# Attention mixing turned round: probabilities as the moving operand, value tiles of 32 columns for four heads held stationary, denominators from a ones tile, inverted by Ln and Exp on ScalarE

## The reference

```python
qk = einsum('bceqd,bcekd->bceqk', q, k) / sqrt(h)
a = softmax(qk, axis=-1)
o = einsum('bceqk,bcekd->bceqd', a, v)
...
x = x + _conv(_mcl(o, Wo, bo), o_conv_w, o_conv_b, 0)
```

## Time and profile before

| | us |
|---|---|
| median of 3 runs | 1269.8 (1269.31 to 1272.35) |
| profiled execution | 1263.9 |
| its span | 1262.0 |
| PE busy | 1106.7 |
| DVE busy | 965.2 |
| POOL busy | 874.2 |
| ACT busy | 655.4 |

### The profile page before, as it was taken

How to read it: one execution, slowest core, us unless ns; L and a number is a source line. 1 busy time by engine, 2 the same in 40 slices (tenths; PEclk the granted TensorE clock), 3 DMA queues, 4 the chain that set the end, 5 groups by cost and what they waited for, 6 DMA issues and landing times. The chain is left out here.

```text
span 1262.0 us, 30504 instructions
## 1 busy us (share of the span) xinstructions
PE 1106.7 (88%) x12696; PEld 752.7 (60%) x12696; DVE 965.2 (76%) x1466; ACT 655.4 (52%) x1078; POOL 874.2 (69%) x812
## 2 busy tenths in 40 slices
PE   0299999999893888999999999999999589999997
PEld 0177777777672145666667666666667444455553
DVE  3789899999763998988898888988873385544344
ACT  1555555555332176666666666666666223346345
POOL 0467777777584499988998888988889005947900
PEclk9899999999897599999999999999989899999999
DMA  9825234331654455445352707162000499975661
GB/s 303 254 79 153 87 111 121 98 111 47 139 132 124 66 89 142 69 79 94 81 97 58 122 28 143 34 115 57 27 19 18 130 365 316 269 256 161 194 208 54
DMA packets 137778, 159.30 MB, mean 126 GB/s; under 512 B 17853, under 2 KB 85709, under 8 KB 137641
## 3 DMA queue, kind: packets, MB, share of 16 engines
q1 hardware_dynamic: 113448, 119.37, 38.8%
q10 hardware_dynamic: 15648, 28.81, 6.5%
q0 software_dynamic: 8544, 9.18, 2.7%
HBM read 106.48 MB, written 52.89 MB: 126 GB/s over the span
## 5 line engine op out<-in xcount | busy, mean ns | idle before, releaser
L1106 POOL TENSOR_TENSOR a_pl<-a_prob 128x512 bf16<-128x512 f32 x416 | 452.0, 1113 | 54.8 <-ACT a_prob L1063 50.7
L1063 ACT ACTIVATE a_prob<-a_col 128x512 f32<-128x512 f32 x512 | 303.0, 597 | 187.2 <-PE a_col L953 176.3
L1007 DVE TENSOR_REDUCE a_negmax<-a_row 128x1 f32<-128x512 f32 x512 | 336.6, 694 | 48.1 <-PE a_row L931 47.6
L710 POOL TENSOR_TENSOR f_yl<-f_y,f_yh 128x768 bf16<-128x768 f32 x80 | 132.8, 1679 | 93.0 <-ACT f_yh L657 93.0
L970 PE MATMUL a_mix<-a_vp,a_prob 128*128 128x65 bf16 x2048 | 195.5, 195 | 1.1 <-DVE a_o L1032 0.9
L970 PEld LDWEIGHTS a_mix<-a_vp,a_prob 128*128 128x128 bf16 x2048 | 163.7, 99 | 53.5 <-issue 5.2
L971 PE MATMUL a_mix<-a_vp,a_pl 128*128 128x65 bf16 x2048 | 193.9, 195 | 0.0
L971 PEld LDWEIGHTS a_mix<-a_vp,a_pl 128*128 128x128 bf16 x2048 | 146.4, 99 | 60.4 <-issue 4.4
L657 ACT ACTIVATE f_yh<-f_y 128x768 bf16<-128x768 f32 x80 | 67.4, 844 | 138.9 <-DVE f_y L548 120.2
L450 PE MATMUL f_acc<-f_wh,f_xh 128*32 128x384 bf16 x1280 | 109.9, 332 | 28.0 <-DVE f_wl L538 25.9
L931 PE MATMUL a_row<-k,q 96*128 96x512 bf16 x256 | 108.3, 429 | 29.0 <-PEq L202 15.0
(11 more groups left out here) (153 smaller groups left out, 2356.8 us busy)
## 6 DMA issues: line engine op xcount, KB each, us to landing
X<-b_x ACTq DMA_DIRECT2D x16, 526.0 KB, 8.2
q<-in_x SPq DMA_DIRECT2D x8, 1024.0 KB, 7.5
a_v<-V SPq DMA_DIRECT2D x16, 512.0 KB, 4.4
Z<-a_z ACTq DMA_DIRECT2D x32, 256.0 KB, 2.7
b_z<-Z SPq DMA_DIRECT2D x16, 512.0 KB, 11.2
b_x<-in_x SPq DMA_DIRECT2D x32, 256.0 KB, 9.9
b_res<-X SPq DMA_DIRECT2D x38, 208.0 KB
out<-b_y ACTq DMA_DIRECT2D x38, 208.0 KB
```

The source lines that it names most:

```text
L710: nc.gpsimd.tensor_tensor(yl[half][n % 2][:], y[half][:], yh[half][n % 2][:], ALU.subtract).then_inc(yl_done, 1)
L1007: nc.vector.reduce_max(negmax[u][:, QT * h + qt:QT * h + qt + 1], row[row_buffer(h, qt)][:], AX.X, negate=True).then_inc(max_done, 1)
L1063: nc.scalar.activation(prob[head % PROBS][:, kt, :], col[kt % 2][:], ACT.Exp).then_inc(exp_done, 1)
L1106: nc.gpsimd.tensor_tensor(pl[head % PROBS][:, kt, :], prob[head % PROBS][:, kt, :], ph[head % PROBS][:, kt, :], ALU.subtract).then_inc(lo_ ...
```

## The change

- `mix_step` becomes `mix_set`. A set is one key block of four heads (4 steps). For each head the stationary operand is a 128 x 32 tile, and the 512 probabilities of that key block move. The four heads of a quad write to partitions 0-31, 32-63, 64-95, 96-127 of one PSUM tile. First come 8 matmuls with a tile of ones (ph and pl of four heads) into `weight`, then 12 with values (vh with ph, vl with ph, vh with pl) into `mix`. Four sets make a quad: features of four heads on the partitions, queries along the free axis.
- `weight` and `mix` have one PSUM buffer each; before, `mix` had two.
- DVE's `invert` and `norm` per head become, per quad, Ln of `weight` on ACT (`log_weight`), Exp of its negative (`invert`) and one 128 x 512 multiplication on DVE (`divide`), straight into `oT`. An activation table set with both functions is loaded ahead.
- The product of the low parts (vl with pl) is left out; before, it was made.
- The tail loses the fp32 turn of `o` and the two copies to `oT`: 8 matmul parts instead of 16 and two ACT operations instead of four.
- `split_max` loses its cast: the high part is read in place.
- DVE still makes 6 of 32 low parts, now every fifth step. Slots: `EXP` 42, `MIX` 54, `KEEP` (Ln, Exp, divide) 67 and 83, `TAIL` 85 to 93.
- Steps are ordered so that four heads of a key block follow one another (`tile_of`). Loads, their order and their bytes are unchanged.

```diff
+        mix = ps("a_mix", [P, W])
+        weight = ps("a_weight", [P, W])
...
+        KEEP = MIX + QUAD * (QT - 1) + 1
+        TAIL = KEEP + QUAD * QT + 2
...
+            def mix_set(n, g):
+                kt, quad = g % QT, SETS // QT * n + g // QT
+                p = (SETS * n + g) % RING
+                pe.wait_ge(lo_pool, pool_lows(n, g))
+                pe.wait_ge(lo_dve, dve_lows(n, g))
+                if n == g == 0:
+                    pe.wait_ge(ones_set, 1)
+                if kt == 0 and quad:
+                    pe.wait_ge(logged, quad)
+                for part in (ph, pl):
+                    for r in range(QUAD):
+                        nc.tensor.matmul(weight[r * DH:(r + 1) * DH, :], ones[:], part[p][:, r, :],
+                                         start=kt == 0 and part is ph, stop=kt == QT - 1 and part is pl)
+                if g == 0:
+                    pe.wait_ge(v_lo, n + 1)
+                if kt == 0 and quad:
+                    pe.wait_ge(divided, quad)
+                for j, (vv, part) in enumerate(((vh, ph), (vl, ph), (vh, pl))):
+                    for r in range(QUAD):
+                        h = g // QT * QUAD + r
+                        last = nc.tensor.matmul(mix[r * DH:(r + 1) * DH, :], vv[n % 2][:, kt, h * DH:(h + 1) * DH], part[p][:, r, :],
+                                                start=kt == j == 0, stop=kt == QT - 1 and j == 2)
                 last.then_inc(mixed, 1)
...
-                    if j < FH:
-                        last = nc.tensor.matmul(out[:, at], o[u % 2][:, part, n, j * P:(j + 1) * P], ident[:], start=n == 0, stop=n == 1)
...
+                for f in range(FH):
+                    last = nc.tensor.matmul(out[:, at], wo[n % CHANNELS][:, f, j * P:(j + 1) * P], oT[n % 2][:, f, at], start=f == 0, stop=f == FH - 1)
...
-                nc.vector.tensor_copy(high, negmax[u][:]).then_inc(max_hi, 1)
...
+            def divide(n, m):
+                quad = SETS // QT * n + m
+                if m == 0 and n >= 2:
+                    ve.wait_ge(out_full, FH * (n - 1))
+                ve.wait_ge(mixed, QT * (quad + 1))
+                ve.wait_ge(inverted, quad + 1)
+                nc.vector.tensor_tensor(oT[n % 2][:, m, :], mix[:], inverse[quad % 2][:], ALU.mult).then_inc(divided, 1)
+
+            pipeline(steps(0, row_max) + units(SPLIT, split_max) + lows(EXP + 1, low_part, False) + quads(KEEP, divide))
...
+            act.preload_act_table_set("natural_log_exp_and_others")
...
+            def log_weight(n, m):
+                quad = SETS // QT * n + m
+                act.wait_ge(mixed, QT * (quad + 1))
+                nc.scalar.activation(logs[quad % 2][:], weight[:], ACT.Ln).then_inc(logged, 1)
+
+            def invert(n, m):
+                quad = SETS // QT * n + m
+                act.wait_ge(logged, quad + 1)
+                if quad >= 2:
+                    act.wait_ge(divided, quad - 1)
+                nc.scalar.activation(inverse[quad % 2][:], logs[quad % 2][:], ACT.Exp, scale=-1.0).then_inc(inverted, 1)
...
+            pipeline(quads(KEEP, log_weight) + units(TURN + 1, keep_max) + units(TURN + 2, load_max) + units(EXP - 2, v_high) + steps(EXP, exp) + quads(KEEP, invert)
+                     + tails(TAIL + QT, keep_out) + tails(TAIL + QT + 1, store_z))
```

More of the change, by code:

```diff
@@ L749, in attend @@
         ident16 = sb("a_ident16", [P, P], BF16)
-        o = [sb(f"a_o{s}", [P, QT, 2, F]) for s in range(2)]
+        ones = sb("a_ones", [P, DH], BF16)
         q = [q0, sb("a_q1", [SHIFTED, HEADS, QT, CHANNELS, P], BF16)]
@@ L916, in _ @@
             sp.dma_start(centre[:], T["centre"]).then_inc(mixing_in, 16)
-            for i in range(1, ITERATIONS):
+            for i in range(1, C // CHANNELS):
                 load(i)
@@ L922, in _, with row_scores @@
         def _(pe):
[L923 to L931, removed]
+            def row_scores(n, t):
+                step, s, m = STEPS * n + t, entry(n), n % CHANNELS
+                h, qt = t // QT, t % QT
+                if m == 0 and t % (QT * HALF) == 0:
+                    pe.wait_ge(qk_in[s][h // HALF], 16 * QK_LOADS * (n // PAIR + 1))
+                if step >= ROWS:
+                    pe.wait_ge(max_done, step - ROWS + 1)
+                nc.tensor.matmul(row[step % ROWS][:].rearrange("p (t w) -> p t w", t=QT), q[s][0:QK_ROWS, h, qt, m, :], k[s][0:QK_ROWS, h, :, m, :],
@@ L954, in col_scores @@
                                  start=True, stop=True).then_inc(col_full, 1)
[L956 to L970, removed]
-                    last = nc.tensor.matmul(mix[h % 2][:, qt, :], pl[p][:, kt, at], vpart, start=False, stop=kt == QT - 1)
+            def mix_set(n, g):
[20 more added lines that the diff above has]
+                                                start=kt == j == 0, stop=kt == QT - 1 and j == 2)
@@ L972, in mix_step, with tail @@
                 last.then_inc(mixed, 1)
-            def tail(i, u, j, part):
-                unit = UNITS * i + u
+            def tail(n, j, part):
                 at = slice(part * PART, (part + 1) * PART)
@@ L1000, in _, with row_max @@
             nc.vector.tensor_copy(ident16[:], ident[:]).then_inc(ident16_set, 1)
[L1001 to L1005 removed]
+            nc.vector.memset(ones[:], 1.0).then_inc(ones_set, 1)
+            def row_max(n, t):
+                step = STEPS * n + t
                 ve.wait_ge(row_full, step + 1)
[L1007 removed]
@@ new lines, in load_max, with exp @@
+            def load_max(n):
+                act.wait_ge(max_kept, n + 1)
+                act.dma_start(q[entry(n)][QK_ROWS:SHIFTED, :, :, n % CHANNELS, :], maxrows[n % PAIR][:]).then_inc(max_in[n % PAIR], 16)
+            def exp(n, t):
+                step = STEPS * n + t
+                sets_done = step // QUAD
+                if t % QUAD == 0 and sets_done >= RING:
+                    act.wait_ge(mixed, sets_done - RING + 1)
+                act.wait_ge(col_full, step + 1)
+                nc.scalar.activation(prob[sets_done % RING][:, t % QUAD, :], col[step % 2][:], ACT.Exp).then_inc(exp_done, 1)
@@ L1086, in _ @@
+            for j in range(FH):
+                act.wait_ge(z_stored[j], 16 * UNITS)
         @block.gpsimd
```

283 lines of the change are left out of this document (118 added, 165 removed).

## The result

| | before | after |
|---|---|---|
| median, us | 1270.4 (1269.31 to 1272.35, 4 runs) | 1256.0 (1250.15 to 1258.79, 4 runs) |
| span of the profiled execution | 1262.0 | 1256.9 |
| `front`, to the end of its last engine | 406.5 | 413.1 |
| `attend`, first k block cleared to last store | 587.5 | 570.8 |
| of it: first Exp to last low part | 537.6 | 529.2 |

The ratio is 0.9879 (95% 0.9841 to 0.9916): 14 us faster, inside the range, and well short of the 36 us forecast. `attend` gained 16.7 us, and the comparison is made there.

The account below looks back on a forecast made before the run. PE was taken to set the pace in the tail slots, DVE in the others. Gains of 26 us over 14.3 units, 8.7 at the end and 1.3 from the table load made 36: 1269.8 to 1234 us, range 1208 to 1264.

Parts of the forecast that it names:

- PE's own costs: In a mixing set on PE, groups of four 512-column matmuls take 0.21 us; a set with two width changes 1.27.
- Rival C: In the mixing, strided `ph` as moving operand costs double: 0.64 us more a set, 1293 us in all; chance 0.06.
- D: In the mixing, loads of the 32-column tiles don't hide: 0.55 us more a set, 1283 us in all; chance 0.03.
- E: On ACT, the table is reloaded between Exp and Ln: + 5 us a unit, 1300 us and above; chance 0.03.
- stall of `divide`: On DVE, each division waits for the last set, Ln and Exps: 0.4 us each, 0.8 a unit.
- POOL's floor: POOL's lows and `v_low` need 30.1 us a unit, the least period; if reached, 30.1 to 31.2, chance 0.22.
- in the other 23 slots ... DVE sets the pace: In a unit's 23 slots without tail parts, DVE needs 21.9 us against PE's 17.5 and sets the pace.
- ACT ... 22.2 to 23.4, with room: ACT's work in a unit: two copies go, four operations like an Exp come, 22.2 to 23.4 us, with room.
- forecast of 32.35: Period of a unit in `attend`: 10.65 + 21.9 + 0.8 us, less 1.0 across the border, against 34.16.
- The end: From the last low part to the last store: 9.0 us in place of 17.7, a gain of 8.7.
- B: In `attend`, bursts, a sinking clock and `divide` stalls eat the gain: period 33.5 to 34.2, 1255 to 1261 us; chance 0.16.
- B's sign: DVE idle before its row maxima for over 3 us a unit, with PE in the mixing.

Follow-up runs that it names:

- i1: Changed kernel without the 8 ones matmuls of a set, ACT copying `mix` in place of Ln, two column buffers; period 30.51 us.
- i2: i1 with the freed PSUM bank as a third buffer of column scores; period 30.65 us.
- f3: Changed kernel with low parts made for 384 of 512 columns, on POOL and DVE; steady period 33.20 us.
- h1: Changed kernel with Ln waiting only for the ones matmuls, inversion following at once, `v_high` a slot earlier; ratio 0.976 to the kernel before, period 32.28 us.
- e4: Changed kernel with each row maximum taken over 256 of 512 scores; steady period 33.20 us, mean 33.39.
- e1: Changed kernel with the tail starting two slots later; ratio 0.9904 to the kernel before, period 33.69 us.
- e2: Changed kernel with each set in two bursts, value matmuls two slots after the ones matmuls; ratio 0.9818 to the kernel before, period 33.19 us.
- f2: Changed kernel with Ln and inverting Exp on 64 of 512 columns, division by a constant tile; period 32.95 us.
- f4: Changed kernel without the product of vl with ph, 4 of 20 matmuls of a set; period 32.36 us.

## The prediction, step by step: what held, and the step that failed

**PE's own costs held.** Groups of four 512-column matmuls start every 0.21 to 0.24 us, the same for ones and values; a group with `pl` takes 0.21 to 0.23, one with `ph` 0.22 to 0.24. Rival C, whose price was to exceed 0.15 a group, was nil. No room is left for weight loads (D): the load of each of the four 32-column tiles is hidden. The Trainium skill ("TensorE: Matmul & The Clock Gate", Part 3) lets loads overlap only where row groups differ; all tiles here use all rows, and the measurement decides against it. A change of width costs what it was given, 643.86 - 643.54 = 0.32 and 645.96 - 645.65 = 0.31 where a group takes 0.22, and a set with both changes 1.23 + 0.10 = 1.33, against 1.27. There is one table load (E):

```profile
412.64 1.28 ACT L1037 ACT_TABLE_LOAD   x1 [10.58 <-PEq L202]
```

**Operations on ACT, DVE and POOL held**, within 500 to 900 us:

```profile
L1108 POOL TENSOR_TENSOR a_pl<-a_prob 128x512 bf16<-128x512 f32 x312 | 331.1, 1089 | 31.8 <-ACT a_prob L1059 31.3
L1012 DVE TENSOR_REDUCE a_negmax<-a_row 128x1 f32<-128x512 f32 x383 | 249.2, 682 | 51.8 <-PE a_row L939 50.9
...
L1023 DVE TENSOR_TENSOR a_pl<-a_prob 128x512 bf16<-128x512 f32 x72 | 92.7, 1288 | 0.0
...
L1031 DVE TENSOR_TENSOR a_oT<-a_mix,a_inverse 128x512 f32<-128x512 f32 x24 | 16.4, 685 | 4.2 <-ACT a_inverse L1071 4.1
...
L1071 ACT ACTIVATE a_inverse<-a_logs 128x512 f32<-128x512 f32 x24 | 15.0, 626 | 0.0
L1064 ACT ACTIVATE a_logs<-a_weight 128x512 f32<-128x512 f32 x23 | 13.7, 597 | 18.4 <-PE a_mix L983 18.4
```

The division takes 0.685 (0.68 forecast), Ln and its inverse 0.60 and 0.63, a low on POOL 1.09 (1.08). DVE's low came out at 1.29 for 1.25, its split at 0.18 for 0.97. The stall of `divide` was 4.1 us in 24, 0.17 each, where 0.4 was taken. DVE's whole need came out at 28.6 us a unit (344.6 in 400), for 28.4. POOL's floor, 30.1 to 31.2, is borne out by i1 and i2 at 30.5 and 30.65.

**What failed is the step "in the other 23 slots ... DVE sets the pace".** It held PE's need of 17.5 us there against DVE's 21.9 and took the difference as slack, as if an engine could fill its sum at any time. (POOL's 22.2 in these slots is above DVE's 21.9; the prediction let it lag, and f3 bears that out.) PE and ACT are chained by two column buffers, and a burst of 1.23 us with nothing in it for ACT opens a gap each time that both must work off. A plain set lasts 3.33, not 3.1; and "ACT ... 22.2 to 23.4, with room" had no price in it, though ACT's operations between bursts cost PE time: each set with Ln and inversion got 0.52 and 0.59 us shorter in h1, the one with `v_high` 0.61. e4 and f3 show that neither DVE nor POOL paced the unit, h1 that the loop did. PE's wait at the head of the tail for the division (8.8 us in 400, 0.7 a unit) had no price in the sum either, but e1 took it away and gained nothing. The period fell by 0.9 us (34.16 to 33.24) instead of 1.8; over 14.3 units that is 13 us in place of 26. With the loop loosened (h1) it is 32.28, next to the forecast of 32.35. That is luck, not the sum come true: h1's DVE is late by a low part of 2.04 us beside `v_low`, where the sum had 1.25 for each.

**A once-only loss was not in the sum.** From the first Exp to the fourth split of the block went 90.2 us, against 85.6 before. From the second split to the third it is 33.1 against 29.4, where the tail, now one unit earlier, falls and none did before. From the third to the fourth it is 36.1 against 35.5, and 2.9 more than a unit takes later, for the maxima's DMA lands late, in this row of PE:

```profile
507.92 0.38 PE L960 MATMUL a_col<-a_q,a_k 98*128 98x512 bf16 x1 [2.45 <-DMA a_q<-a_maxrows]
```

Behind this stand PE's granted clock is 0.50 from 509.16 to 512.50, where it was 1.00 up to 507.92. From the fourth split to the last low part 13.0 us were gained, 11.5 in twelve units and 1.5 behind the last split, where the prediction had nothing; less the 4.6 this is the 8.4 of the middle, 537.6 - 529.2. e2 is free of the long unit (33.2) at the same period, and in h1 it takes 38.1; why two bursts avoid it was not tried by itself.

**The end: right in mechanism, a little off in size.** Last low to last store is 10.8 us for 9.0, a gain of 6.9 for 8.7. The rows, to be held against the earlier trace rows:

```profile
959.80 13.36 POOL L1108 TENSOR_TENSOR a_pl<-a_prob 128x512 bf16<-128x512 f32 x12
...
974.56 0.60 ACT L1064 ACTIVATE a_logs<-a_weight 128x512 f32<-128x512 f32 x1 [4.28 <-PE a_mix L983]
...
976.66 3.68 PE L997 MATMUL a_out<-a_oT,a_wo 128*128 128x128 f32 x16 [2.15 <-DVE a_oT L1031]
981.12 2.05 PE L997 MATMUL a_out<-a_oT,a_wo 128*128 128x128 f32 x16 [0.78 <-ACT a_z L1077]
...
983.92 0.33 ACTq L1081 DMA_DIRECT2D Z<-a_z  x1
```

The first 16 tail matmuls took 3.68 us, the next 16 2.05. PE had stood 2.15 us for Ln, inversion and division, and the stretches give the granted clock of each (the number behind POOL's):

```profile
976.66:980.38 3.72, 3.68 (x16) 3.48 (x16) 0.00 (x0) 0.00 (x1) 0.00 (x0) 0.54 0.00 0
981.12:983.20 2.08, 2.05 (x16) 1.86 (x16) 0.00 (x0) 0.00 (x0) 0.00 (x0) 1.00 0.33 126
```

The first group ran at 0.54, near the lower level of 1.2 GHz, the second at 2.4; that is 1.6 of the 1.8 us by which the end was longer than forecast. The table load gave 1.4 us for 1.3. Attention in all: 8.4 + 6.9 + 1.4 = 16.7 us.

**The rivals.** B is the nearest, by its time (1255 to 1261; its period, 33.5 to 34.2, lies above the 33.24 measured) and by its sentence that bursts eat the gain; but it put the loss into DVE without row scores, a sinking clock and long stalls of `divide`. The clock is 1.00 over the 400 us, but for the 3.3 us behind the late DMA, and the stalls were 0.17 us. DVE did stand idle before its row maxima for more than the 3 us a unit that was B's sign (50.9 us in 400, 4.2 a unit), but it did so before the change as well (42.5, or 3.6), and with half maxima, where it waits 161.8 us, the period is the same. B was given 0.16 for a mechanism that isn't there, and the one that is had no place among the rivals.

## What to carry to other kernels

When small matmuls are gathered into a burst, ask of every engine that PE feeds how long its buffers last through it: sums of busy time by stretch don't show a loop through a double buffer, waits in both directions between two engines that are not full do. Work of the starved engine then belongs into the burst, where most of it is hidden (h1: 1.7 us of a unit's sets from a change of order alone). When one limit gives way the next is measured by relieving both, not one at a time; and the next can be a collision that only the new order brings about, which no sum of means contains.

## What was not expected of the hardware

- DVE's reciprocal of 128 x 512 from PSUM takes 3.34 us, five times a multiplication of that size (0.685).
- A DVE low part takes 0.67 us by itself and up to 1.50 beside one of POOL; the mean rose from 1.12 to 1.29 with nothing in the operation changed. Where a low part of DVE and `v_low` of POOL meet, the one that started second waits for the first: in f2, f4 and h1 the low part started second, took 2.65, 2.61 and 2.04 us, and ended 0.54 to 0.56 us behind `v_low`. After the change `v_low` starts second and rose from 2075 ns to this:

```profile
L1102 POOL TENSOR_TENSOR a_vl<-a_v,a_vh 128x1024 bf16<-128x1024 f32 x12 | 30.3, 2524 | 9.1 <-ACT a_vh L1043 9.1
```

Its output has another layout (a tile of its own instead of columns of `vp`), but that is not the reason: in h1 the layout is the same as after, and the mean is 2136 ns:

```profile
L1104 POOL TENSOR_TENSOR a_vl<-a_v,a_vh 128x1024 bf16<-128x1024 f32 x13 | 27.8, 2136 | 0.0
```

- A moving bf16 operand with a stride of two elements costs at most 0.02 us in a group of four 512-column matmuls.
